# Sparse attention with RWKV channel mixing: query gathers one group ahead, and another order in the tail

## The reference

```python
q, k, v = heads(x @ Wq + bq), heads(x @ Wk + bk), heads(x @ Wv + bv)
scores = einsum('bhqd,bhkd->bhqk', q, k) / 4
sparsity = scores.max(-1) - scores.mean(-1)
top_idx = top_k(sparsity, 307)                  # for each batch and head
attn = softmax(q[top_idx] @ k.T / 4)
out = zeros.at[top_idx].set(attn @ v)
x = layernorm(x + out @ Wo + bo)
r = sigmoid(mix_r(x, x_prev) @ W_r)             # x_prev: the token before
kk = square(relu(mix_k(x, x_prev) @ W_k))
return layernorm(x + r * (kk @ W_v))
```

## Time and profile before

| | us |
|---|---|
| median of 3 runs | 3500.51 |
| the profiled execution, its own time | 3496.0 |
| its span, first to last instruction | 3494.2 |
| VectorE busy | 3028.1 (87%) |
| TensorE busy (matmuls, ends modelled) | 3092.9 (89%) |
| ScalarE busy | 2788.8 (80%) |
| GpSimd busy | 1473.1 (42%) |
| last main step's maximum (L973) ends | 3107.4 |
| last `put` begins | 3326.6 |

### The profile page before, as it was taken

The page is one execution under the profiler, slowest core; times in us unless marked ns, Lnnn a source line. Parts: engine busy times, 40 slices in busy tenths (PEclk is TensorE's granted clock), DMA queues, the critical chain, the costliest instruction groups (busy, mean ns, idle before and its releaser), DMA issues.

```text
span 3494.2 us, 58455 instructions
## 1 busy us (share of the span) xinstructions
PE 3092.9 (89%) x15873; PEld 1424.2 (41%) x15873; DVE 3028.1 (87%) x6406; ACT 2788.8 (80%) x5893; POOL 1473.1 (42%) x2567
## 2 busy tenths in 40 slices
PE   5999999997799998998899978899988999876688
PEld 3334333342244433433443434444344443344366
DVE  2889988899988899899899998889998889965478
ACT  3889888897789998898799966799866899843555
POOL 2210022100136543433454535766456664258754
PEclk8999999999999999999999999999999999988799
DMA  6431232317122251141112152221521224021022
GB/s 181 149 81 35 61 85 76 83 34 17 25 38 38 38 33 32 26 32 32 33 33 42 26 32 46 54 38 32 27 52 30 51 38 32 7 20 22 14 74 72
DMA packets 262292, 163.60 MB, mean 47 GB/s; under 512 B 167563, under 2 KB 241483, under 8 KB 257867
## 3 DMA queue, kind: packets, MB, share of 16 engines
q1 hardware_dynamic: 255819, 158.50, 26.2%
q0 software_dynamic: 6144, 1.37, 0.5%
HBM read 111.86 MB, written 47.86 MB: 46 GB/s over the span
## 4 chain that ended last, share of the span: by engine, by line
PE 30%; DVE 24%; ACT 23%; issue 19%; POOL 2%; DMA 1%; SPq 0%; ACTq 0%; DVEq 0%; POOLq 0%
ACT AB L834 17%; DVE JK L973 14%; PE CP L568 9%; PE DP L572 9%; ACT E L855 4%; DVE msk L1008 3%; PE PV L679 1%; DVE SPr L973 1%; PE PV L680 1%; PE BP L664 1%; PE PV L516 1%; DVE fst L1119 1%; PE BP L516 1%; DVE VF L1157 1%; PE BP L702 1%
## 5 line engine op out<-in xcount | busy, mean ns | idle before, releaser
L973 DVE CUSTOM_DVE_ANT_0 JK<-DP,AB 128x1024 bf16<-128x1024 f32 x2048 | 2465.5, 1222 | 266.4 <-ACT AB L834 89.4
L834 ACT ACTIVATE AB<-CP 128x512 f32<-128x512 f32 x4096 | 2229.4, 598 | 379.4 <-PE CP L568 319.3
L568 PE MATMUL CP<-KS,QS 128*128 128x512 f16 x4096 | 1391.7, 386 | 71.2 <-issue 16.3
L572 PE MATMUL DP<-KS,QS 128*128 128x512 f16 x4096 | 1237.2, 384 | 123.1 <-DVE SPr L973 103.6
L1338 POOL TENSOR_TENSOR SCR<-E 128x307 f16<-128x307 f32 x928 | 649.7, 710 | 606.6 <-ACT E L855 601.2
L568 PEld LDWEIGHTS CP<-KS,QS 128*128 128x128 f16 x4096 | 391.2, 97 | 805.5 <-ACT AB L834 651.9
L572 PEld LDWEIGHTS DP<-KS,QS 128*128 128x128 f16 x4096 | 339.7, 98 | 519.8 <-DVE SPr L973 333.9
L855 ACT ACTIVATE E<-BP 128x307 f32<-128x307 f32 x871 | 379.5, 436 | 44.0 <-PE BP L664 39.0
L1201 POOL TENSOR_SCALAR SCR<-SCR 128x48 f16<-128x48 f16 (+2 forms) x122 | 50.1, 411 | 578.8 <-DVE SCR L941 321.6
L664 PE MATMUL BP<-QT,KA 128*128 128x307 f16 x871 | 258.4, 297 | 18.8 <-ACT QT L847 18.5
L679 PE MATMUL PV<-E,XT 128*128 128x307 bf16 x512 | 161.7, 316 | 25.1 <-POOL SCR L1338 24.8
(11 more groups left out here) (336 smaller groups left out, 2800.5 us busy)
## 6 DMA issues: line engine op xcount, KB each, us to landing
KS<-KTC SPq DMA_DIRECT2D x256, 128.0 KB
QS<-QSC SPq DMA_DIRECT2D x512, 64.0 KB
KA<-KTC SPq DMA_DIRECT2D x128, 128.0 KB
QN<-SCR SPq DMA_DIRECT2D x16, 544.0 KB, 3.4
SCR<-in_L_attn_x SPq DMA_DIRECT2D x16, 512.0 KB, 6.6
KTC<-SCR SPq DMA_DIRECT2D x32, 256.0 KB, 2.2
QSC<-SCR SPq DMA_DIRECT2D x32, 256.0 KB, 2.4
AO<-E SPq DMA_DIRECT2D x2, 4096.0 KB, 22.2
```

What stands on the lines that cost most here:

```text
L568: pe.matmul(o, qs, ks[j][:, 1, :], start=True, stop=True).then_inc(sc_c, 1)
L572: r = pe.matmul(o[:, 512 * j:512 * j + 512], qs, ks[j][:, 0, :], start=True, stop=True)
L834: act.activation(AB[p % 3][:, 512 * j:512 * j + 512], BANK["C%d" % j], ACT.Abs).then_inc(ab_full, 1)
L973: dve.tensor_tensor_reduce(out=JK[p % 2][:], in0=BANK["D%d" % u], in1=AB[p % 3][:], scale=1.0, scalar=-3.0e38, op0=ALU.add, op1=ALU.max, a ...
```

## The change

The queries' places become a ring over all heads (`hx % 8`), with one landing semaphore for each of four heads in turn. A group's first `gath` and `arr` leave `attend` and go into a new generator `prelude`, which the selection runs right after its group's index list; in the tail `prelude` gathers and arranges all heads of the group, without gaps. `attend` begins with its steps at once and keeps the bank P if the next group is already ahead. Keys are loaded one head ahead over group borders too. The last two groups have 3 and 3 heads where they had 4 and 2. In the tail, attention gets two steps after each `cmp` and one after every other selection token; as long as the search of the last group runs, all subtractions go to GpSimd and no background step is taken while attention holds P. The bank C1 joins the spare ones in the tail.

```diff
-GROUPS = [(0, 0, 8), (0, 8, 5), (0, 13, 3), (1, 0, 5), (1, 5, 5), (1, 10, 4), (1, 14, 2)]
+GROUPS = [(0, 0, 8), (0, 8, 5), (0, 13, 3), (1, 0, 5), (1, 5, 5), (1, 10, 3), (1, 13, 3)]
...
+    def prelude(g):
+
+        n = GROUPS[g][2] if tail[0] else 1
+        gaps = 0 if tail[0] else 1
+        yield [("ka", 0), ("qgzero",)] if g == 0 else []
+        for h in range(n):
+            yield [("gath", g, h)]
+        for _ in range(5 * gaps):
+            yield []
+        for h in range(n):
+            yield [("arr", g, h)]
+        for _ in range(4 * gaps):
+            yield []
+        ahead[g] = n
+
     def attend(g):
         n = GROUPS[g][2]
-        gaps = 0 if tail[0] else 1
-        yield [("ka", g, 0)] + ([("qgzero",)] if g == 0 else [])
-        for _ in range(5 * gaps):
-            yield None
-        yield [("gath", g, 0)]
-        for _ in range(4 * gaps):
-            yield None
-        yield [("arr", g, 0)]
-        for _ in range(4 * gaps):
-            yield None
         while state["open"]:
             yield None
-        spare.remove("P")
+        if "P" in spare:
+            spare.remove("P")
...
-                    if hl + 1 < n:
-                        step.append(("ka", g, hl + 1))
-                if kc == 10 and hl + 1 < n:
+                    if HEAD0[g] + hl + 1 < NB * H:
+                        step.append(("ka", HEAD0[g] + hl + 1))
+                if kc == 10 and ahead[g] <= hl + 1 < n:
...
-                if kc == 18 and hl + 1 < n:
+                if kc == 18 and ahead[g] <= hl + 1 < n:
...
-                step.append(("st", g, hl, kc, bank(), "D" if tail[0] and kc % 2 else "G"))
+                step.append(("st", g, hl, kc, bank(), "D" if tail[0] and kc % 2 and not state["search"] else "G"))
...
     def attention():
         for g in range(len(GROUPS)):
-            while ("s", g) not in done or (g == G1 and "v1" not in done):
+            while g not in ahead or (g == G1 and "v1" not in done):
                 yield None
             yield from attend(g)
-            spare.append("P")
+            if g + 1 not in ahead:
+                spare.append("P")
             done.add(g)
...
+            state["search"] = True
             yield from select(g)
-            done.add(("s", g))
+            state["search"] = False
+            yield from prelude(g)
...
-    spare += ["D00", "D01", "D10", "D11"]
+    spare += ["D00", "D01", "D10", "D11", "C1"]
     while not set(range(len(GROUPS))) <= done:
-        s = next(sel, None)
-        plan.extend(s or [])
-        for _ in range(1 if s else 2):
+        step = next(sel, None) or []
+        plan.extend(step)
+        for _ in range(2 if step and step[0][0] == "cmp" else 1):
             plan.extend(next(att, None) or [])
-        plan.extend(next(back, None) or [])
+        if "P" in spare or not state["search"]:
+            plan.extend(next(back, None) or [])
...
             def gath(g, h):
...
                 if h == 0:
                     pool.wait_ge(l_i, 64 * (g + 1))
                     pool.wait_ge(l_m, 32 * HEAD0[g + 1])
-                    after(pool, q_pool, arranged[0])
+                if hx >= 8:
+                    pool.wait_ge(q_pool, arranged[hx - 8])
                 for c, (_, w) in enumerate(CH):
...
-                        out=QG[0:w, k, :], out_offset=None, in_=QNr[b],
-                        ...).then_inc(l_g, 16)
+                        out=QG[0:w, 3 * (hx % 8) + c, :], out_offset=None, in_=QNr[b],
+                        ...).then_inc(l_g[hx % 4], 16)
...
             def arrange(g, h):
...
-                pool.wait_ge(l_g, 48 * (HEAD0[g] + h + 1))
-                after(pool, ah_pe, HEAD0[g])
+                pool.wait_ge(l_g[hx % 4], 48 * (hx // 4 + 1))
+                after(pool, ah_pe, hx - 7)
```

More of the change, by code:

```diff
@@ L58, in schedule @@
     spare = ["B", "P", "D00", "D01", "D10", "D11"]
-    state = {"turn": 0, "open": None}
+    state = {"turn": 0, "open": None, "search": False}
     tail = [False]
     done = set()
+    ahead = {}
     def bank():
@@ L289, in schedule @@
     plan.append(("tail",))
[L290 removed]
+    spare += ["D00", "D01", "D10", "D11", "C1"]
     while not set(range(len(GROUPS))) <= done:
[L292 to L294 removed]
+        step = next(sel, None) or []
+        plan.extend(step)
+        for _ in range(2 if step and step[0][0] == "cmp" else 1):
             plan.extend(next(att, None) or [])
[L296 removed]
+        if "P" in spare or not state["search"]:
+            plan.extend(next(back, None) or [])
     for step in back:
         plan.extend(step)
[L299 removed]
+    spare.append("C0")
     for step in feed(1, True):
@@ L412, in attention_rwkv @@
         BQ, BK, MR, MK, SH, MR1, MK1, KB = (slice(2 * i, 2 * i + 2) for i in range(8))
-        l_w, l_z, l_m, l_i, l_g, l_q = (sem(n) for n in ("l_w", "l_z", "l_m", "l_i", "l_g", "l_q"))
+        l_w, l_z, l_m, l_i, l_q = (sem(n) for n in ("l_w", "l_z", "l_m", "l_i", "l_q"))
+        l_g = [sem(f"l_g{i}") for i in range(4)]
         l_s, l_k, l_o, l_a = ([sem(f"{n}{i}") for i in range(2)] for n in ("l_s", "l_k", "l_o", "l_a"))
@@ L652, in qt @@
                 for c, (a, w) in enumerate(CH[:2]):
-                    pe.transpose(o[:, a:a + w], QST[0:w, 3 * hl + c, :], identh[0:w, 0:w])
-                pe.transpose(o[:, 256:256 + CH[2][1] + 1], QST[0:52, 3 * hl + 2, :], identh[0:52, 0:52]).then_inc(ah_pe, 1)
+                    pe.transpose(o[:, a:a + w], QST[0:w, 3 * (hx % 8) + c, :], identh[0:w, 0:w])
+                pe.transpose(o[:, 256:256 + CH[2][1] + 1], QST[0:52, 3 * (hx % 8) + 2, :], identh[0:52, 0:52]).then_inc(ah_pe, 1)
                 owed[bank] = ((ah_act, hx + 1),)
@@ L1299, in qgzero @@
                 pool.wait_ge(q_pool, seq.mark(pool.memset(QST, 0.0)))
-            arranged = [0]
+            arranged = []
             def gath(g, h):
                 b = GROUPS[g][0]
+                hx = HEAD0[g] + h
                 ixf = idxs[g][:].rearrange("p h c -> p (h c)")
@@ L1312, in gath @@
                     pool.indirect_dma_start(
-                        out=QG[0:w, k, :], out_offset=None, in_=QNr[b],
-                        in_offset=bass.IndirectOffsetOnAxis(ap=ixf[0:w, k:k + 1], axis=0)).then_inc(l_g, 16)
+                        out=QG[0:w, 3 * (hx % 8) + c, :], out_offset=None, in_=QNr[b],
+                        in_offset=bass.IndirectOffsetOnAxis(ap=ixf[0:w, k:k + 1], axis=0)).then_inc(l_g[hx % 4], 16)
             def arrange(g, h):
-                a = slice(3 * h, 3 * h + 3)
+                hx = HEAD0[g] + h
+                a = slice(3 * (hx % 8), 3 * (hx % 8) + 3)
                 q = QG[:, a, 0:DH]
@@ L1327, in arrange @@
                 dup(z[3], z[2])
-                arranged[0] = seq.mark(pool.tensor_scalar(mr, m, -0.5 / MC, 0.0, ALU.mult, ALU.add))
-                pool.wait_ge(q_pool, arranged[0])
+                arranged.append(seq.mark(pool.tensor_scalar(mr, m, -0.5 / MC, 0.0, ALU.mult, ALU.add)))
+                pool.wait_ge(q_pool, arranged[hx])
                 pool.wait_ge(q_pool, seq.mark(pool.tensor_copy(mz[0], mr)))
@@ L1539, in ixdma, with ka @@
                     sp.dma_start(idxs[g][0:w, 0:n, c], IDX[g, 0:n, a0:a0 + w].rearrange("h s -> s h")).then_inc(l_i, 16)
-            def ka(g, hl):
-                hx = HEAD0[g] + hl
+            def ka(hx):
                 b, h = divmod(hx, H)
```

## The result

The change makes the kernel slower: 3517.25 us in the median of 6 runs (3510.61 to 3522.26) against 3498.64 (3494.19 to 3500.78, also 6), a ratio of 1.0054, 95% interval 1.0041 to 1.0067. Forecast were 3461 us and a range of 3434 to 3494. The profiled execution took 3517.4, its span 3515.6.

What follows compares the result with a forecast made beforehand. The prediction took VectorE's work per slot to bound the main loop and GpSimd's queue the tail. Main loop +19 us and tail -58 us made -39: 3500.5 - 39 = 3461 us, range 3434 to 3494.

Steps and rivals of the forecast that it cites:

- the second of the main loop: Main loop: `feed(0)` begins earlier, putting 42 slots beside selection (+17 us) and nine outside a search (+1 us).
- Point 5: Main loop: early gathers' waits, at most 7.8 us, are covered by `pv`'s lag of 8.3 us; nothing added, 39 us if uncovered.
- No change* rival: Main loop borders: early gathers stop GpSimd for all of their 39 us, giving 3500 us; chance 0.07.
- Point 3: Main loop's end: `feed(0)` finishes before group 4, the last 14 slots hold group 5's attention alone: -7 us.
- point 4: Main loop: select(5) starts a head earlier, with 3 heads instead of 4 and the same 128 slots: nothing.
- Point 1: Main loop: attention of group 0 starts earlier and gaps after groups 0 and 1 close, 37 slots: +9 us.
- the other term of point 2: Main loop: 13 more `feed(0)` slots beside select(4), when group 3 ends earlier; forecast 5 us for slots 1488 to 1792.
- 66.9 + 5.4 + 24.5 + 7.4: Tail until group 5's last `put`: GpSimd's search queue, two drained pipelines, `prelude` of group 6, group 5's last 11 steps.
- smaller gain* rival: Tail: TensorE's lower clock slows group 6 by up to 18 us, perhaps with slower subtractions: 3474 to 3493; chance 0.2.
- The *slower* one: Tail search: counts queue behind `pv` waiting for GpSimd, rounds take 5.6 us, giving 3517 us; chance 0.08.
- signs of being wrong: A round over 3.5 us, L973 ending after 3140, or GpSimd idle over 10 us in the tail except for the index list.
- The rule on shared interfaces: Tail search: if VectorE's compares slow GpSimd's 62 subtractions through shared SBUF interfaces, 13 us more, 3474.

Runs made afterwards that it cites:

- Run 1: The changed kernel with each selected head's two maxima writes sent behind every second search round instead of all in one block: 3495.01 us, ratio 0.9992.
- run 5: Run 1 plus the loads of the first three tiles of `feed(0)` sent together seven slots ahead: 3486.8 us, ratio 0.9974.
- run 2: The kernel before the change, with group 3's block of ten maxima writes moved into the running `feed(0)`, behind search round 8: 3496.05 us, ratio 1.0.
- run 6: The kernel before the change, with the maxima writes spread over the search's rounds, as a control: 3493.89 us, ratio 0.9994.
- run 12: The changed kernel with only `prelude`'s first gather moved four slots later: 3513.11 us, ratio 1.0054.
- run 10: Run 5 with the early loads four slots ahead instead of seven: 3487.83 us, ratio 0.9977.
- run 11: Run 10 with `prelude`'s first gather four slots later, as many slots in all: 3467.83 us, ratio 0.9922.
- run 4: The changed kernel, but in the tail every other subtraction goes to VectorE during the last search too: 3514.95 us, ratio 1.0051.
- run 7: The kernel before the change, with the changed kernel's tail order alone: 3505.15 us, ratio 1.0033.
- run 3: The changed kernel with `feed(0)` begun 32 slots later, leaving 24 of its steps for the tail: 3517.73 us, ratio 1.0065.
- run 8: Run 1 with the last two groups of 4 and 2 heads, as before the change: 3508.56 us, ratio 1.0041.
- run 9: The changed kernel with only the early loads of `feed(0)`, seven slots ahead, maxima writes still in one block: 3512.96 us, ratio 1.0052.

## Why the prediction was wrong

**The step that failed** is the second of the main loop. It priced "29 of those slots lie beside select(3)" at 1.89 - 1.49 us each, the mean of 100 slots of the stage. `feed(0)` did not only run beside select(3), it started there. At its start the loads have no lead: in after's timelines SyncE issues the first at 1982.18 and TensorE, after 6.64 us of waiting, begins the first transpose at 1984.93 (before's own start had such a wait of 2.74 us, inside the mean); later ones stand behind ten writes on SyncE's queue. Of SyncE's queue the forecast had looked at the keys only. Run 1 takes the second standstill away and run 5 the first as well: the slots concerned shrink by 24.9 and 11.3 us, and what stays of the stretch is +13.9 against +13. Runs 2 and 6 show that the block does not matter at another place in the running stage, nor its spreading in before. The block was to be seen in the trace of before.

**Point 5, "I take nothing"**, was wrong too. The 8.3 us of cover were the lag of `pv`. In slots 968 to 976 that cover failed: to the 8.39 us of waiting come the three gathers themselves, 12 us on GpSimd's queue in all, and `pv` waited 4.82. At the border of slots 1792 to 1808 `feed`'s mixing stands behind the gather on GpSimd, and it has no such lag. The two places lost 7.5 and 8.1 us in after, where the forecast had 0, and the later gather gives 7.4 and 2.0 of them back (run 12). On the repaired kernel it was worth 20 us (runs 10 and 11). That is the *No change* rival's mechanism at part of its price. Open is why run 12 loses elsewhere what it wins at the borders, and why the early loads make the border at 1792 dearer: its list wait is 7.8 to 8.9 us with them and 4.7 in after, but no run varies the distance by itself.

**Point 3's -7 came, and point 4's "nothing" did not.** The last 14 slots (2033 to 2047) take 18.6 us instead of 27.8, 9.2 less. But slots 1808 to 2033 take 12.1 more. Select(5) starts 64 slots earlier and takes its one-hot and index work along, now beside attention. In before that work filled the last slots (2024 to 2047: 40.8 us, 1.77 a slot), in after it fills slots 1960 to 1984 (42.9 us, 1.79 a slot). Windows of the maximum in these parts, before and then after:

```profile
3071.00:3106.10 35.10, 23.40 (x40) 1.00 0.03 8
```

```profile
3060.00:3092.10 32.10, 22.04 (x37) 0.95 0.01 1
```

So slots with this work cost nearly the same whatever runs beside them. The forecast took their cost away at the end and put nothing for their new place. This is read from traces; no run tests it.

**Point 1 and the other term of point 2.** Select(4)'s slots cost +4.0 against 5. Closed gaps read +5.7 against 9, but that is no confirmation: the gather's wait in slots 968 to 976 alone is 7.5 of it, so the rest is about -2. With the later gather (run 12) slots 960 to 1040 take 4.0 us more than before's, what 16 closed slots at 0.25 should; slots 1040 to 1312 are shorter than before's in every variant of after (by 4.1 us in after), which point 1 had not foreseen.

**The tail: the number was right, its reason only in part.** 167.2 against 161.0. By parts: from the tail's start to group 5's last `put` (3282.38) 103.0 us, forecast 66.9 + 5.4 + 24.5 + 7.4 = 104.2. Group 6 took 23.9, 21.4 and 18.9, together 64.2 against 56.8. The 7.4 us beyond are the *smaller gain* rival's, in part: at the first head, in a window from 3290 to 3298 with a clock of 0.80, GpSimd's subtractions of every other step start 1.54 us apart (0.70 for the subtraction and 0.84 of waiting, in the rows above) instead of 0.86. But the forecast summed GpSimd's queue for the search (66.9 us), and run 4 takes 14 us off that queue without shortening anything; what set the stretch instead no run isolates. Runs 7, 3 and 8 show what the shorter tail consists of: the order gives nothing, a `feed` step that leaves the tail gives 0.9 us, and the new group sizes give 13.5 to 20.6. As an estimate, 37 steps and 20.6 less the order's 8 make 46 of the 52 us.

**The rivals.** The *slower* one forecast 3517 and the kernel took 3517, by chance: it asked for a search round over 5.3 us, and rounds take 2.9 us on average. Its mechanism, a count behind `pv` that waits for GpSimd, shows clearly in the round of 7.0 us alone. Two of the forecast's own signs of being wrong did come, L973's end after 3140 and three rounds over 3.5 us. The rule on shared interfaces (the Trainium skill, GPSIMD Engine Reference, "1. Specifications") speaks of VectorE instructions in a 2-port mode or with two SBUF inputs. Of 58 subtractions, of which most ran beside compares, none took over 0.770 us, so the 13 us that it would have cost did not come. For VectorE's subtraction, which has two inputs, the traces agree: in run 4's tail the 32 subtractions on GpSimd that overlap one of VectorE's for half their time or more take 0.93 us in the median, the 38 that overlap none 0.70; in before it is 0.93 (40) and 0.70 (38).

**The range.** It allowed 30 us for the main loop at most, from mean rates of the stages. Run 11 has a main loop of +27 and a tail of -56, and lands at 0.9922, 27 us under before where 39 were forecast. The remaining 12 are 8 in the main loop, 2 in the tail, and the rest behind the last `put` (169.3 against 167.6).

## What to carry to other kernels

When a stage is moved to another time, price its start apart from its steady rate: walk every in-order queue at the new place and ask what stands ahead of its first transfers, before they have a lead. The same queue block can be free in the running stage and cost its whole length at the start. Where a wait is moved ahead on an in-order engine, its cover is the lag of the nearest consumer of anything queued behind it, and the transfers behind the wait count too. And a sum over one engine's queue that comes out right does not show that the queue sets the time: take work off it and see.

## What the runs showed of the hardware

Ten writes of 8 KB from columns of SBUF to single 4-byte elements of HBM rows held SyncE's queue for 23.7 us in after, and for 21.7 to 29.9 us in before and in runs 2, 3 and 9, while the DMA share of after read 1.3 to 1.5 at 3 GB/s; the load behind them was issued only when they were out. In pairs they took 3.4 to 3.7 us a pair. A list of indices, written to HBM and read back before an indirect gather, took 8.4 to 9.1 us from the first issue to the gather. A subtraction on GpSimd took 0.70 us alone or beside VectorE's compares, and 0.90 to 0.93 (medians of after, before and run 4) beside VectorE's subtractions.
